# A graph network layer on one core: the normalise steps of the first stage in batches of eight blocks, the statistics further ahead, and x in twenty slots

## The chip, the cores and the metric

The kernel runs on 1 core of one Trainium2 chip. The metric is device time in microseconds (us) of one execution, lower is better.

## The reference, cut to what matters

`x` has 50,000 rows (nodes) of 128 features, and there are 12,500 edges (`src`, `dst`, sorted by `dst`), each with 3, 5 and 32 attributes. In the reference `rbf`, `pij` and `dij` are the edges' attributes, and each `_resmlp` is a two layer residual block of 128x128 matrices with its own weights.

```python
h = jnp.maximum(_layernorm(x, axis=-1), 0.0)
...
xx = _resmlp(h, ...[0])
xs, xp, xd = (_resmlp(h, ...[i])[idx_j] for i in (1, 2, 3))
s = xx + segment_sum(gs * xs, idx_i)
p = segment_sum(gp * xp[:, None, :], idx_i)
d = segment_sum(gd * xd[:, None, :], idx_i)
...
y = s + (pa * pb).sum(-2) + (da * db).sum(-2)
return x + _resmlp(y, ...[4])
```

The change lies in the first stage alone: `h`, the first MLP on every node, and the sorting of the edges.

## The kernel before, in words

The kernel has three stages that follow each other on every engine: `first_stage` (L265), `edge_phase` (L1014) and `final_stage` (L843).

**Work of the first stage.** The rows of x come in 98 blocks of 512 rows (`NB`, L93; `TB` = 4 rows in each of 128 partitions). For each block, x is loaded (`load_x`, L334, SP queue), VectorE takes the statistics of its four row groups (`stats`, L479, four `bn_stats`), a batch of blocks gets mean, 1/deviation and bias by 20 small VectorE instructions (`norm_step`, L488; LN_OPS = 20), and the rows are normalised and rectified: half by VectorE (`centre`, L537, and `rectify`, L548), half by ScalarE (`norm`, L699), except around the one-hots, where ScalarE does all four (`by_scalar`, L315). The block is stored as h (`store_h`, L350), TensorE transposes it (L780) and runs three layers (L795, L804, L811) with ScalarE's activations between (L723, L733, L739), and ScalarE copies the result out (L746) for `store` (L342).

**The sort.** Beside this the same engines sort the edges by source in two passes, first by the low digit, then by the high one. A pass starts with `digits` (L558) and 98 `onehots` (L587, VectorE), 49 in each of two steps; TensorE counts them (L755). Then 14 chunks of seven tiles follow, one every 2.5 steps: TensorE adds up running counts (L768), VectorE takes seven `picks` (L602, four in one step and three in the next) and one rank instruction (L619), and POOL scatters the rows to DRAM (L431), paced by TensorE's progress. Pass 0 has its one-hots at steps 0 and 1 and its chunks from step 4, pass 1 at steps 49 and 50 and from step 53 (`passes`, L271). Before pass 1, POOL reads the sorted edges back to SBUF in one DMA of 2 MB (L465), and `digits` of pass 1 waits for it (L565).

**What sets the order.** Every engine's program is written out by hand in steps k. On VectorE (L640 to L669) step k is: centre block k + 1; the statistics of the block or blocks of `stats_at(k)` (L299), with one norm step after each `bn_stats` from k = 7 on; rectify block k + 1, after the first block's statistics; the picks, then digits and one-hots, with norm steps between; and the norm steps left over. `stats_at(k)` is block k + 9 in the steady state. `norm_steps_at(k)` (L305) spreads the 20 steps of a batch of four blocks that begins at block b over k = b - 5 to b - 2, five a step. The centring of a block also waits for the transposition of the block four before it and for the store of that block's h (L543, L544).

x has 14 slots (`NX`, L96). Fourteen loads are issued at the start, the last six behind the loads of the edges (L380). Later, step k of SP stores h of block k, stores the result of block k - 4 and then loads block k + 12 (L407), whose slot was freed by block k - 2. So a block's x is asked for in SP's step k and its statistics stand in VectorE's step k + 3.

```python
            batches = [(0, 2), (2, 2)] + [(b, min(4, NB - b)) for b in range(4, NB, 4)]
...
                    if 0 <= k - 4 < NB:
                        store(k - 4)
                    if NX <= k + 12 < NB:
                        load_x(k + 12)
```

Of the kernel before, what the change touches and what calls it, by code (L numbers as in the profile page):

```python
# [76 lines left out]
def gnn_kernel(nc, x, src, dst, attr3, attr32, attr5, w_rs, w_rp, w_rd, w_pp, w_pd,  # L77
# [6 lines left out]
    P = 128  # L84
# [6 lines left out]
    TB = 4  # L91
    BLOCK = TB * P
    NB = -(-N // BLOCK)  # L93


    NX = 14  # L96
    CH = 7
    OH = 49
    T = -(-E // P)
# [25 lines left out]
    with ctx:  # L125
        def sb(name, shape, dt=fp32):
            return ctx.enter_context(nc.sbuf_tensor(name, shape, dt))
# [40 lines left out]

        xin = sb("xin", [P, NX, TB, F])
        yin = sb("yin", [P, 4, TB, F])  # L170
# [19 lines left out]
        def psb(name, shape, dt=fp32):  # L190
            return own.enter_context(nc.sbuf_tensor(name, shape, dt))
# [13 lines left out]
        upto = psb("upto", [P, LOW])  # L205
# [5 lines left out]
        earlier = psb("earlier", [P, CH, CH])  # L211
        corr = psb("corr", [P, T])
        warm = psb("warm", [P, 1])
        stat = psb("stat", [P, 16, TB, 6])
        lnt = psb("lnt", [P, 2, 6, 4 * TB])
        means = psb("means", [P, 2, 4 * TB])
        rnorm = psb("rnorm", [P, 2, 4 * TB])
        nbias = psb("nbias", [P, 2, 4 * TB])
        padrow = psb("padrow", [P, 3, W])

        groups = []
# [43 lines left out]
        def first_stage():  # L265
# [4 lines left out]
            BANK_A, BANK_COUNT, BANK_RUN, BANK_O = psum[3], psum[4], psum[5], psum[7]  # L270
            passes = (Pass(0, 0, 2, 4, 5, by_low), Pass(1, 49, 51, 53, 54, by_src))  # L271
            LN_OPS = 20
            batches = [(0, 2), (2, 2)] + [(b, min(4, NB - b)) for b in range(4, NB, 4)]

            x_in = [sem(f"n_x_in{i}") for i in range(NX)]
            stored = [sem(f"n_stored{i}") for i in range(4)]
# [22 lines left out]
            def stats_at(k):  # L299

                early = ((2, 3), (4, 5, 6, 7), (8, 9), (10, 11), (12, 13), (14,), (15,))
                blocks = early[k] if k < len(early) else (k + 9,)
                return [b for b in blocks if b < NB]

            def norm_steps_at(k):  # L305


                for B, (b, n) in enumerate(batches):
                    first, steps = ((0, 1), (0, 1), (1, 1), (3, 3))[B] if B < 4 else (b - 5, 4)
                    if B and first <= k < first + steps:  # L310
                        each = -(-LN_OPS // steps)
                        return [(B, i) for i in range(1, LN_OPS + 1) if (i - 1) // each == k - first]
                return []
# [19 lines left out]
            def sync(sp):  # L333
                def load_x(b):  # L334
                    s = b % NX
                    if b >= NX:
                        if by_vector(b - NX + 1):
                            sp.wait_ge(nrm_v, by_vector(b - NX + 1))
                        sp.wait_ge(nrm_a, b - NX + 1)
                    sp.dma_start(xin[:, s, :, :], xb_view(at(b), x)).then_inc(x_in[s], 16)  # L340

                def store(b):  # L342
                    s = b % 4
                    sp.wait_ge(row_done, b + 1)
                    if b == NB - 1:

                        sp.wait_ge(stored[(b - 1) % 4], 16 * ((b - 1) // 4 + 1))
                    sp.dma_start(xb_view(at(b), ysum), rowout[:, s, :, :]).then_inc(stored[s], 16)

                def store_h(b):  # L350
                    s = b % 4
                    sp.wait_ge(nrm_a, b + 1)
                    if by_scalar(b) < TB:
                        sp.wait_ge(nrm_v, by_vector(b + 1))
                    if b == NB - 1:

                        sp.wait_ge(h_stored[(b - 1) % 4], 16 * ((b - 1) // 4 + 1))
                    sp.dma_start(xb_view(at(b), htab), xn[:, s, :, :]).then_inc(h_stored[s], 16)

                load_x(0)  # L360
                load_x(1)
                sp.wait_ge(s_staged, 1)
                assert load_parts(src, st_src[:, :], sp, s_src, 1) == N_SRC
                sp.dma_start(w1_sb[:, m, :], w1[m, :, :]).then_inc(s_w, 16)
                with nc.allow_non_contiguous_dma(reason="biases to partitions"):
                    sp.dma_start(b1_sb[:, :], b1.rearrange("m k -> k m"), allow_slow_non_contiguous=True).then_inc(s_w, 16)
                    sp.dma_start(b2_sb[:, :], b2.rearrange("m k -> k m"), allow_slow_non_contiguous=True).then_inc(s_w, 16)
                load_x(2)
                load_x(3)
                sp.dma_start(w2_sb[:, m, :], w2[m, :, :]).then_inc(s_w, 16)  # L370
                sp.dma_start(wo_sb[:, m, :], wout[m, :, :]).then_inc(s_w, 16)
                for b in range(4, 8):
                    load_x(b)
                sp.wait_ge(s_staged, 2)
                n_rest = 0
                for dram, tile, per in ((dst, st_dst, 1), (attr3, st3, NP3), (attr5, st5, ND5), (attr32, st32, NRBF)):
                    flat = tile[:, :] if per == 1 else tile[:, :, :].rearrange("p t c -> p (t c)")
                    n_rest += load_parts(dram, flat, sp, s_edges, per)
                assert n_rest == N_REST
                for b in range(8, NX):  # L380
                    load_x(b)
                store_h(0)
                store_h(1)
                for k in range(2, NB + 4):
                    if k < NB:
                        store_h(k)
                    if k == 6:
                        sp.wait_ge(s_cst, 4)
                        sp.dma_start(w1_sb[:, m + 1:, :], w1[m + 1:, :, :].rearrange("m k n -> k m n")).then_inc(s_w2, 16)
                        sp.dma_start(w2_sb[:, m + 1:, :], w2[m + 1:, :, :].rearrange("m k n -> k m n")).then_inc(s_w2, 16)  # L390
                        sp.dma_start(wo_sb[:, m + 1:, :], wout[m + 1:, :, :].rearrange("m k n -> k m n")).then_inc(s_w2, 16)
                        sp.dma_start(wpp_sb[:, :], w_pp).then_inc(s_w2, 16)
                        sp.dma_start(wpd_sb[:, :], w_pd).then_inc(s_w2, 16)
                        for j in range(TB):
                            for n, w in enumerate((w_rp, w_rd, w_rs)):
                                sp.dma_start(wr_sb[j * Q:j * Q + NRBF, n, :], w).then_inc(s_w2, 16)
                    if k == 10:
                        for row, parts, each in groups:
                            sp.dma_start(by_src[row:row + parts * each, :].rearrange("(p t) w -> p t w", t=each),
                                         padrow[0:parts, 0:each, :]).then_inc(s_init, 16)  # L400
                        for lo in range(0, SPARE, TB):
                            n = min(TB, SPARE - lo)
                            sp.dma_start(ysum[N + lo * P:N + (lo + n) * P, :].rearrange("(t p) f -> p t f", p=P),
                                         zeros[:, 0:n * F].rearrange("p (t f) -> p t f", t=n)).then_inc(s_init, 16)
                    if 0 <= k - 4 < NB:
                        store(k - 4)
                    if NX <= k + 12 < NB:  # L407
                        load_x(k + 12)
                for s in s_scat:
                    sp.wait_ge(s, 2 * 16 * CHUNKS)  # L410
                sp.wait_ge(s_init, 16 * (-(-SPARE // TB) + len(groups)))
                with nc.allow_non_contiguous_dma(reason="one word of each row"):
                    for g in (0, 1):
                        load_group(sp, by_src, er, rb, nxt, g, g, TB, T, rows_in[g])
# [63 lines left out]
            def vector(dve):  # L478
                def stats(b, lo, hi):  # L479
                    s = b % NX  # L480
                    if lo == 0:
                        dve.wait_ge(x_in[s], 16 * (b // NX + 1))
                    for j in range(lo, hi):
                        last = nc.vector.bn_stats(stat[:, b % 16, j, :], xin[:, s, j, :])  # L484
                    if hi == TB:
                        last.then_inc(st_done, 1)

                def norm_step(B, i):  # L488


                    b, n = batches[B]
                    q, w, at0 = B % 2, n * TB, B * LN_OPS
                    st = stat[:, b % 16:b % 16 + n, :, :].rearrange("p b t c -> p (b t) c")
                    t = [lnt[:, q, i, 0:w] for i in range(6)]
                    mean, r, nb = means[:, q, 0:w], rnorm[:, q, 0:w], nbias[:, q, 0:w]
                    V_ = nc.vector
# [30 lines left out]
                    elif i == 19:  # L527
                        if B >= 2:
                            last = batches[B - 2][0] + batches[B - 2][1]
# [110 lines left out]
                for k in range(NB):  # L640
                    blocks, todo, pick = stats_at(k), norm_steps_at(k), picks_at(k)
# [1062 lines left out]
```

## Time and profile before

| what | value |
|---|---|
| median of 3 runs | 1262.18 us (1259.76 to 1266.66) |
| the profiled execution's own time | 1264.56 us |
| its span, first to last instruction | 1262.7 us |
| mean granted TensorE clock | 0.963 |
| VectorE busy in the span | 660.6 us (52%) |
| TensorE busy | 1135.0 us (90%) |
| first stage | from 0 to about 453 us of the span |

Busy shares are averages over three stages with different limits. A timeline row gives an instruction's start and duration, and in brackets the idle time of its engine before it and what ended that. The chain that ended last is followed back from the last instruction to what released each; "issue" in it is time without a cause that the profile shows. A wait for several semaphores is put down to the last of them by the profile, and the ends of matmuls are modelled.

### The profile page before, as it was taken

The numbers are of one execution on the slowest core, as the hardware profiler recorded it, in microseconds if no ns is written. First come the engines' busy times: TensorE is split into PE (matmuls) and PEld (weight loads), VectorE is DVE, ScalarE is ACT, GpSimd is POOL, SyncE is SP. The second block draws the span as 40 slices with busy tenths as digits, with TensorE's granted clock in tenths as the row PEclk, the third lists the DMA queues.
The fourth block names the chain that finished last, engine by engine and source line by source line (L and its number), as shares of the span: only waits on it lengthen the run. The fifth ranks groups of instructions, "written<-read, shape, count | busy, mean of one in ns | idle before, by whom it ended". The sixth has DMA issues, their size and how long they took to land.

```text
span 1262.7 us, 23295 instructions
## 1 busy us (share of the span) xinstructions
PE 1135.0 (90%) x6835; PEld 766.0 (61%) x6835; DVE 660.6 (52%) x2466; ACT 758.2 (60%) x1425; POOL 456.9 (36%) x423
## 2 busy tenths in 40 slices
PE   2778998797989856999999999999977999999998
PEld 1555665474656533666666666666744666666665
DVE  9866876695778303565556555655541222222222
ACT  2357878656877833555655565556524666666665
POOL 3055666015565531456555655565340000000000
PEclk9889999898999978999999999999988999999999
DMA  7166667735766430233333333333435888788876
GB/s 223 67 213 199 224 213 224 253 129 162 232 217 211 165 89 11 46 57 46 54 55 57 47 54 55 55 49 52 83 55 170 250 263 263 247 266 258 256 257 206
DMA packets 162765, 190.56 MB, mean 151 GB/s; under 512 B 57956, under 2 KB 82444, under 8 KB 162413
## 3 DMA queue, kind: packets, MB, share of 16 engines
q1 hardware_dynamic: 124636, 144.39, 38.4%
q0 software_dynamic: 23920, 19.29, 9.7%
q10 hardware_dynamic: 14112, 25.70, 5.3%
q8 instruction: 47, 0.77, 0.3%
q14 instruction: 50, 0.41, 0.1%
HBM read 93.01 MB, written 96.30 MB: 150 GB/s over the span
## 4 chain that ended last, share of the span: by engine, by line
PE 77%; DVE 11%; issue 7%; DMA 2%; ACT 1%; another core or an unknown queue 1%; SPq 0%; POOL 0%; ACTq 0%; POOLq 0%; DVEq 0%
PE bank L976 7%; PE quad L964 7%; PE bank L1489 5%; PE quad L968 5%; PE bank L1499 5%; PE bank L811 4%; PE quad L795 4%; PE bank L1563 4%; PE bank L1531 3%; DVE onehot L589 3%; PE bank L1564 3%; PE quad L804 3%; PE quad L956 3%; PE quad L780 2%; DVE stat L484 2%
## 5 line engine op out<-in xcount | busy, mean ns | idle before, releaser
L1164 POOL DMA_INDIRECT node_sums<-rowout,row_i x98 | 155.0, 1582 | 199.6 <-ACT rowout L1426 177.1
L900 DVE TENSOR_TENSOR rowout<-bank,xin 128x512 f32<-128x512 f32 x98 | 67.8, 692 | 242.0 <-PE bank L976 242.0
L811 PEld LDWEIGHTS bank<-wo_sb,s 128*128 128x128 f32 x784 | 102.8, 194 | 64.9 <-issue 64.9
L431 POOL DMA_INDIRECT edges_by_src<-pay,rank_i x98 | 96.2, 981 | 111.5 <-DVE rank_i L619 50.6
L431 POOL DMA_INDIRECT edges_by_low<-pay,rank_i x98 | 96.6, 986 | 99.3 <-DVE rank_i L619 42.2
L976 PEld LDWEIGHTS bank<-wo_sb,s 128*128 128x128 f32 x784 | 102.8, 191 | 47.8 <-issue 47.8
L1197 DVE SCALAR_TENSOR_TENSOR h<-bank,b_sb,hT 128x512 f32<-128x512 f32 (+1 forms) x75 | 55.5, 740 | 122.2 <-PE bank L1499 122.2
L484 DVE BATCH_NORM_STATS2 stat<-xin 128x6 f32<-128x128 f32 x392 | 105.4, 284 | 21.9 <-DMA xin<-in_x_dram 21.9
L811 PE MATMUL bank<-wo_sb,s 128*128 128x128 f32 x784 | 106.0, 279 | 11.0 <-issue 9.0
L72 POOL DMA_INDIRECT yin<-node_h,er x98 | 94.9, 968 | 53.8 <-issue 29.3
L709 ACT ACTIVATE xn<-xin,nbias,rnorm 128x128 f32<-128x128 f32 x210 | 101.8, 492 | 14.3 <-DVE nbias L535 14.3
L607 DVE SCALAR_TENSOR_TENSOR picked<-bank,onehot 128x256 bf16<-128x256 f32 x196 | 75.9, 418 | 62.8 <-issue 39.3
L795 PE MATMUL quad<-s,w_sb 128*128 128x512 f32 x196 | 105.6, 622 | 0.0
L976 PE MATMUL bank<-wo_sb,s 128*128 128x128 f32 x784 | 103.5, 275 | 0.9 <-DVE rowout L900 0.9
L964 PE MATMUL quad<-s,w_sb 128*128 128x512 f32 x196 | 101.4, 599 | 0.4 <-ACT s L919 0.4
L1373 ACT ACTIVATE s<-h 128x512 f32<-128x512 f32 (+1 forms) x75 | 46.6, 622 | 74.5 <-DVE h L1197 74.5
L1489 PE MATMUL bank<-s,w_sb 128*128 128x512 f32 (+1 forms) x150 | 79.9, 615 | 12.2 <-ACT s L1365 9.2
L1405 ACT COPY AB<-bank 128x512 f32<-128x512 f32 x98 | 58.1, 593 | 50.4 <-PE bank L1564 50.2
L780 PE MATMUL quad<-ident,xn 128*128 128x128 f32 x296 | 47.8, 286 | 40.8 <-issue 21.7
L746 ACT COPY rowout<-bank 128x512 f32<-128x512 f32 x98 | 57.5, 587 | 43.6 <-remote 27.8
L919 ACT ACTIVATE s<-quad,b_sb 128x512 f32<-128x512 f32 x98 | 67.3, 687 | 26.3 <-PE quad L964 26.2
L733 ACT ACTIVATE s<-quad,b_sb 128x512 f32<-128x512 f32 x98 | 67.2, 686 | 22.6 <-PE quad L795 14.4
(193 smaller groups left out, 2376.1 us busy)
## 6 DMA issues: line engine op xcount, KB each, us to landing
xin<-in_x_dram SPq DMA_DIRECT2D x196, 256.0 KB, 3.9
node_h<-xn SPq DMA_DIRECT2D x98, 256.0 KB
node_sums<-rowout SPq DMA_DIRECT2D x98, 256.0 KB
yin<-node_sums SPq DMA_DIRECT2D x98, 256.0 KB, 4.0
out_dram<-rowout ACTq DMA_DIRECT2D x98, 256.0 KB, 3.8
border_sums_by_tile<-border_sums SPq DMA_DIRECT2D x24, 256.0 KB, 2.1
pay<-edges_by_low POOLq DMA_DIRECT2D x1, 2058.0 KB, 10.7
edges_by_low<-pay,rank_i POOLq DMA_INDIRECT x98
```

The source lines that it names most:

```text
L72: pool.indirect_dma_start(out=xg[:, s, j, :], out_offset=None, in_=x, in_offset=bass.IndirectOffsetOnAxis(ap=er[:, s, j, 1:2].bitcast(mybi ...
L431: nc.gpsimd.indirect_dma_start(out=ps.dram, out_offset=bass.IndirectOffsetOnAxis(ap=rank_i[:, t:t + 1], axis=0), in_=pay[:, t, :], in_offs ...
L484: last = nc.vector.bn_stats(stat[:, b % 16, j, :], xin[:, s, j, :])
L607: nc.vector.scalar_tensor_tensor(out=picked[:, j, :], in0=BANK_RUN[:, 0:LOW], scalar=1.0, in1=onehot[:, t, :], op0=ALU.mult, op1=ALU.mult, ...
L709: ins = nc.scalar.activation(xn[:, b % 4, j, :], xin[:, s, j, :], ACT.Relu, bias=nbias[:, q, i:i + 1], scale=rnorm[:, q, i:i + 1])
L780: last = nc.tensor.matmul(BANK_X[k % 4][:, j * P:(j + 1) * P], xn[:, k % 4, j, :], ident[:, :], start=j == 0, stop=False, is_transpose=Tru ...
L795: nc.tensor.matmul(BANK_A[:, :], w1_sb[:, m, :], s1[:, (k - 1) % 3, :], start=True, stop=True).then_inc(a_done, 1)
L811: last = nc.tensor.matmul(BANK_O[:, j * P:(j + 1) * P], s3[:, (k - 3) % 3, j * P:(j + 1) * P], wo_sb[:, m, :], start=True, stop=True)
L964: nc.tensor.matmul(BANK_A[:, :], w1_sb[:, m, :], s1[:, s, :], start=True, stop=True).then_inc(a_done, 1)
L976: last = nc.tensor.matmul(BANK_O[:, j * P:(j + 1) * P], s3[:, s, j * P:(j + 1) * P], wo_sb[:, m, :], start=True, stop=True)
L1164: nc.gpsimd.indirect_dma_start(out=ysum, out_offset=bass.IndirectOffsetOnAxis(ap=row_i[:, t % 2, j:j + 1], axis=0), in_=urow[:, t % 2, j, ...
L1489: nc.tensor.matmul(BANK_A[:, 0:e], w1_sb[:, MLP[m], :], s1[:, k % 2, 0:e], start=True, stop=True).then_inc(a_done, 1)
```

## The change

There are four edits, all in `first_stage`.

```diff
-    NX = 14
+    NX = 20
...
-        stat = psb("stat", [P, 16, TB, 6])
-        lnt = psb("lnt", [P, 2, 6, 4 * TB])
+        stat = psb("stat", [P, 32, TB, 6])
+        lnt = psb("lnt", [P, 2, 6, 8 * TB])
...
-            batches = [(0, 2), (2, 2)] + [(b, min(4, NB - b)) for b in range(4, NB, 4)]
+            LARGE = 32
+            batches = [(0, 2), (2, 2)] + [(b, 4) for b in range(4, LARGE, 4)] + [(b, min(8, NB - b)) for b in range(LARGE, NB, 8)]
...
-                blocks = early[k] if k < len(early) else (k + 9,)
+                upto = [k + 9 + min(max(k - 7, 0) // 2, 5) for k in (k - 1, k)]
+                blocks = early[k] if k < len(early) else range(upto[0] + 1, upto[1] + 1)
...
-                    first, steps = ((0, 1), (0, 1), (1, 1), (3, 3))[B] if B < 4 else (b - 5, 4)
+                    first, steps = ((0, 1), (0, 1), (1, 1), (3, 3))[B] if B < 4 else (b - 5, 4) if b <= LARGE else (b - 6, 5)
...
-                    if NX <= k + 12 < NB:
-                        load_x(k + 12)
+                    if NX <= k + NX - 2 < NB:
+                        load_x(k + NX - 2)
```

`means`, `rnorm` and `nbias` grow like `lnt`, and the other places where `stat` is indexed take `% 32`. What the edits do:

- Batches hold eight blocks from block 32 on. Their 20 norm steps stand in VectorE's steps k = b - 6 to b - 2, four a step, and the three steps after that have none. Each works on 32 elements per partition and no longer on 16.
- The statistics run ahead by 14 blocks in place of 9. The lead grows by one block in each of the steps 9, 11, 13, 15 and 17, which take the statistics of two blocks. In return the last five steps that had statistics have none.
- x has 20 slots. Twenty loads are issued at the start, and SP's step k loads block k + 18. A block's x is asked for four steps ahead of its statistics.

The first place is VectorE ahead of the second pass's one-hots: the end of step 48 and step 49. `digit_i` is the first instruction of `digits`. Before:

```order
L484 BN_STATS stat<-xin 128x6
L522 TENSOR_TENSOR lnt<-lnt 128x16
L484 BN_STATS stat<-xin 128x6
L524 TENSOR_TENSOR lnt<-lnt 128x16
L484 BN_STATS stat<-xin 128x6
L526 SCALAR_TENSOR_TENSOR lnt<-lnt 128x16
L484 BN_STATS stat<-xin 128x6
L522 TENSOR_TENSOR lnt<-lnt 128x16
L566 CAST digit_i<-pay 128x98
L568 TENSOR_SCALAR digit_i<-digit_i 128x98
L571 CAST digit_f<-digit_i 128x98
L589 TENSOR_SCALAR onehot<-digits_h,digit_f 128x256 x2
```

Now (two lines more stand above, so line numbers are higher by 2):

```order
L547 TENSOR_TENSOR xn<-xin,means 128x256
L486 BN_STATS stat<-xin 128x6 x4
L556 SCALAR_TENSOR_TENSOR xn<-xn,rnorm 128x256
L547 TENSOR_TENSOR xn<-xin,means 128x256
L486 BN_STATS stat<-xin 128x6 x4
L556 SCALAR_TENSOR_TENSOR xn<-xn,rnorm 128x256
L486 BN_STATS stat<-xin 128x6 x4
L568 CAST digit_i<-pay 128x98
L570 TENSOR_SCALAR digit_i<-digit_i 128x98
L573 CAST digit_f<-digit_i 128x98
L591 TENSOR_SCALAR onehot<-digits_h,digit_f 128x256 x49
```

The steps `lnt<-lnt` between the statistics are gone in steps 47, 48 and 49 and between the one-hots of step 49; step 50 has the first four of the batch at block 56.

The second place is SP's queue at the start: the last load of the edges, the x loads behind it and the first stores of h. Before:

```order
L239 DMA st<-in_edge_attr_dram 15x3136
L239 DMA st<-in_edge_attr_dram 1x1728
L340 DMA xin<-in_x_dram 128x512 x6
L358 DMA node_h<-xn 128x512 x3
L340 DMA xin<-in_x_dram 128x512
L358 DMA node_h<-xn 128x512
```

Now:

```order
L239 DMA st<-in_edge_attr_dram 15x3136
L239 DMA st<-in_edge_attr_dram 1x1728
L342 DMA xin<-in_x_dram 128x512 x12
L360 DMA node_h<-xn 128x512 x3
L342 DMA xin<-in_x_dram 128x512
L360 DMA node_h<-xn 128x512
```

Six more loads of x stand ahead of the first store of h, and each later load is for a block that is six further on.

## Rows read from the trace of the kernel before

**Rows 1.** The page: busy time by engine, and the chain that ended last
```profile
PE 1135.0 (90%) x6835; PEld 766.0 (61%) x6835; DVE 660.6 (52%) x2466; ACT 758.2 (60%) x1425; POOL 456.9 (36%) x423
...
PE 77%; DVE 11%; issue 7%; DMA 2%; ACT 1%; another core or an unknown queue 1%; SPq 0%; POOL 0%; ACTq 0%; POOLq 0%; DVEq 0%
```

**Rows 2.** Timeline of TensorE after the first stage: start, duration, what, [idle before]
```profile
464.91 1.08 PE L1468 MATMUL quad<-ident,yin 128*128 128x128 f32 x4 [12.19 <-DMA yin<-node_h,er]
```

**Rows 3.** Stretches: length, busy PE, PEld, DVE, ACT, POOL, clock, DMA share, GB/s
```profile
225.00:250.00 25.00, 16.00 (x84) 10.57 (x83) 15.26 (x85) 17.60 (x37) 0.59 (x1) 0.87 0.76 275
...
350.00:375.00 25.00, 21.43 (x118) 14.38 (x117) 17.55 (x103) 18.41 (x38) 15.21 (x16) 1.00 0.65 210
```

**Rows 4.** Timeline of VectorE, 225 to 250 us
```profile
225.97 0.42 DVE L545 TENSOR_TENSOR xn<-xin,means 128x256 f32<-128x256 f32 x1
...
227.34 0.29 DVE L484 BATCH_NORM_STATS2 stat<-xin 128x6 f32<-128x128 f32 x1 [0.95 <-DMA xin<-in_x_dram]
...
237.62 0.29 DVE L484 BATCH_NORM_STATS2 stat<-xin 128x6 f32<-128x128 f32 x1 [8.69 <-DMA xin<-in_x_dram]
...
238.74 0.24 DVE L566 CAST digit_i<-pay 128x98 int32<-128x98 f32 x1
...
239.52 0.48 DVE L589 TENSOR_SCALAR onehot<-digits_h,digit_f 128x256 bf16<-128x256 bf16 x2
```

**Rows 5.** Timeline of the SP queue, same stretch
```profile
224.68 0.40 SPq L340 DMA_DIRECT2D xin<-in_x_dram  x1
...
227.72 0.69 SPq L340 DMA_DIRECT2D xin<-in_x_dram  x1
```

**Rows 6.** The reload of the sorted edges: POOL's timeline, and issue to landing
```profile
225.90 0.59 POOL L465 DMA_DIRECT2D pay<-edges_by_low  x1 [2.40 <-DMA edges_by_low<-pay,rank_i]
...
pay<-edges_by_low POOLq DMA_DIRECT2D x1, 2058.0 KB, 10.7
```

**Rows 7.** Timeline of TensorE around the one-hots of step 49
```profile
239.14 0.66 PE L780 MATMUL quad<-ident,xn 128*128 128x128 f32 x4 [0.31 <-ACT xn L709]
...
239.63 1.02 PE L795 MATMUL quad<-s,w_sb 128*128 128x512 f32 x2
...
249.35 1.04 PE L755 MATMUL bank<-onehot,ident_h 128*128 128x256 bf16 x4 [8.69 <-DVE onehot L589]
```

**Rows 8.** The chain that ended last, 223 to 300 us: start, duration, what
```profile
250.88 9.22 DVE onehot L589 x47
...
260.15 5.52 PE bank L755 x49
```

**Rows 9.** Timeline of VectorE: statistics alone, with a step between, and two picks
```profile
52.17 0.86 DVE L484 BATCH_NORM_STATS2 stat<-xin 128x6 f32<-128x128 f32 x4
...
92.65 0.42 DVE L607 SCALAR_TENSOR_TENSOR picked<-bank,onehot 128x256 bf16<-128x256 f32 x1 [0.99 <-PE bank L768]
...
114.35 0.42 DVE L607 SCALAR_TENSOR_TENSOR picked<-bank,onehot 128x256 bf16<-128x256 f32 x1 [1.18 <-issue]
...
154.65 0.29 DVE L484 BATCH_NORM_STATS2 stat<-xin 128x6 f32<-128x128 f32 x1
...
154.94 0.28 DVE L484 BATCH_NORM_STATS2 stat<-xin 128x6 f32<-128x128 f32 x1
```

**Rows 10.** The stretch 12 to 16 us, columns as in Rows 3
```profile
12.00:16.00 4.00, 1.09 (x4) 0.71 (x4) 3.93 (x24) 2.73 (x7) 0.00 (x0) 1.00 1.04 291
```

**Rows 11.** Timeline of VectorE in the first one-hot stage
```profile
14.31 0.47 DVE L589 TENSOR_SCALAR onehot<-digits_h,digit_f 128x256 bf16<-128x256 bf16 x2
...
23.29 5.36 DVE L589 TENSOR_SCALAR onehot<-digits_h,digit_f 128x256 bf16<-128x256 bf16 x9
```

**Rows 12.** Timeline of ScalarE in the second pass: a late copy
```profile
333.27 0.59 ACT L746 COPY rowout<-bank 128x512 f32<-128x512 f32 x1 [1.93 <-remote]
```

**Rows 13.** Timeline of TensorE in the second pass, after an idle stretch
```profile
311.24 0.63 PE L780 MATMUL quad<-ident,xn 128*128 128x128 f32 x4 [2.13 <-issue]
...
311.71 1.84 PE L795 MATMUL quad<-s,w_sb 128*128 128x512 f32 x2
```

More of the change, by code:

```diff
@@ L213, in gnn_kernel @@
         warm = psb("warm", [P, 1])
-        stat = psb("stat", [P, 16, TB, 6])
-        lnt = psb("lnt", [P, 2, 6, 4 * TB])
-        means = psb("means", [P, 2, 4 * TB])
-        rnorm = psb("rnorm", [P, 2, 4 * TB])
-        nbias = psb("nbias", [P, 2, 4 * TB])
+        stat = psb("stat", [P, 32, TB, 6])
+        lnt = psb("lnt", [P, 2, 6, 8 * TB])
+        means = psb("means", [P, 2, 8 * TB])
+        rnorm = psb("rnorm", [P, 2, 8 * TB])
+        nbias = psb("nbias", [P, 2, 8 * TB])
         padrow = psb("padrow", [P, 3, W])
@@ L483, in stats @@
                     for j in range(lo, hi):
-                        last = nc.vector.bn_stats(stat[:, b % 16, j, :], xin[:, s, j, :])
+                        last = nc.vector.bn_stats(stat[:, b % 32, j, :], xin[:, s, j, :])
                     if hi == TB:
@@ L492, in norm_step @@
                     q, w, at0 = B % 2, n * TB, B * LN_OPS
-                    st = stat[:, b % 16:b % 16 + n, :, :].rearrange("p b t c -> p (b t) c")
+                    st = stat[:, b % 32:b % 32 + n, :, :].rearrange("p b t c -> p (b t) c")
                     t = [lnt[:, q, i, 0:w] for i in range(6)]
```

## The prediction

> **What bounds the kernel now.** I read the page first. TensorE is busy 90% of the span and 77% of the chain that ended last; VectorE is busy 52% and has 11% of that chain [rows 1]. The change adds and removes nothing on TensorE, so what it can move is TensorE's idle time in the first stage. The handover at the stage's end keeps nothing back: the next stage's first transposition comes 12.19 us after TensorE's last work, behind stores, loads of edge rows and a gather that all follow the last block [rows 2]. Time won in the first stage is time won in all.
>
> Next I read stretches of the first stage. In one from the second pass VectorE is busy 17.55 us of 25 and TensorE 21.43. In 225 to 250 us TensorE has its worst stretch of the sorting time, 16.00 of 25, at a mean granted clock of 0.87, with DMA at 0.76 [rows 3].
>
> The timelines say why. VectorE centres block 49 at 225.97 and does the statistics of step 48 at 227.34. Then it waits 8.69 us, to 237.62, for the x of block 58. Then come four statistics with four norm steps between, `digits` at 238.74 and the first one-hot at 239.52 [rows 4]. That x was asked for at 227.72 [rows 5], so it took 9.9 us; the median over the kernel is 3.9 (the page's DMA issues). Two us earlier, at 225.90, POOL had asked for the 2 MB of sorted edges, which took 10.7 us [rows 6]. TensorE transposes block 50 at 239.14, does a little more and then waits 8.69 us for the one-hots of step 49, to 249.35 [rows 7]. The chain runs through both sets of one-hots and the second set's counts [rows 8]. So the one-hots' start at 239.52 sets the rest of the stage, and each us off it is a us won.
>
> **The change, part by part.**
>
> *The x of step 49 comes earlier.* The statistics of step 49 are now those of block 63, whose load stands in SP's step 45. That is the load at 224.68, where block 57 stood before, and not the one at 227.72 [rows 5]. Block 57's data let VectorE go on at 227.34, so it landed in 2.7 us [rows 4, 5], issued 1.2 us ahead of the reload [rows 6]. VectorE then has nothing to wait for until `digits`, which waits for the reload: 225.90 + 10.7 = 236.6 [rows 6]. Four statistics without steps take 0.86 us [rows 9], so even with centring and rectifying before them they end near 229. `digits` moves from 238.74 to 236.6: 2.1 us. That is far less than the 8.69 us of the wait, because the reload is late next, 1.0 us ahead of where the x had been. The 1.1 us of statistics and steps that stood behind the wait now lie under the reload's.
>
> *The norm steps.* From block 32 on there were 17 batches and are now 9, so 8 x 20 = 160 instructions go. One step between two statistics stretches their distance from 0.86 / 4 = 0.21 us to 154.94 - 154.65 = 0.29 us [rows 9], so it costs 0.08 us, and 160 come to 12.8 us. The steps that stay from there on, 9 x 20, are longer, since they work on 32 elements and not on 16: 16 more are at most 16/256 of a centring of 256 elements, 0.42 us [rows 4], so 0.03 us each and some 5 us in all, an estimate. So VectorE loses some 8 us of work. What of it is on the path? One step among the first set of one-hots is: 0.1 us. The others lie where VectorE waits for TensorE: it waits for running counts ahead of nearly every chunk, for instance 0.99 and 1.18 us [rows 9], and most other such waits in the second pass are longer. I take 0.1 us. The bounds are 0 and, if all of the second pass were on VectorE's path, 4 us: steps 53 to 86 had 34 x 5 = 170 norm steps and now have 88; 82 x 0.08 = 6.6, less 88 x 0.03 = 2.6.
>
> *The statistics further ahead.* Five steps of the first pass take four more statistics each, 0.86 us [rows 9], 4.3 us together. In the steps 9, 11, 13, 15 and 17 they stand in front of a wait for TensorE: of the five waits the two shortest are 0.99 us (step 11) and 1.18 us (step 16, behind step 15) [rows 9], both longer than 0.86. I take 0; the upper end is 4.3. The last five steps without statistics give nothing back, since VectorE has time there.
>
> *Six more loads at the start.* They add 6 x 256 KB to a queue that moves 291 GB/s [rows 10], so 5.3 us of transfers, and six issues ahead of the first store of h. The edges' loads stand ahead of them and are not delayed. h is needed by nobody before block 4. Does a busy DMA slow VectorE? At a DMA share of 1.04 [rows 10] two one-hots take 0.47 us [rows 11], which is their time at 239.52 as well, 0.48 [rows 4]. But nine of them at 23.29 took 5.36 us [rows 11], where 9 x 0.2 = 1.8 was due. The DMA was busy then too, and POOL was copying the edges. I take 0, by the row with the same DMA share and no POOL work. If it was the DMA, 5.3 us more at a third of the pace cost 3.5 us; that is the upper end.
>
> *More slots in the steady state.* The loads per step are the same three transfers, so shares don't change; an earlier x only matters where VectorE waits for it, which outside the stretch above happens off the path.
>
> **The sum.** -2.1 (x under the reload) - 0.1 (a step) = -2.2 us. Against the profiled execution's own time, 1264.56, that is 1262.4 (span 1260.5). That execution was 2.4 us above the median of the three runs, 1262.18; against the median it is 1260.0.
>
> **A rule against the trace.** VectorE's idle time in the second pass [rows 3] and its waits ahead of the picks [rows 9] say that fewer small steps there are worth nothing. The Trainium skill (Perfetto Trace Analysis, section "Optimizing Scalar/DVE Operations") says that each VectorE instruction on SBUF has some 60 ns of fixed overhead and that grouping into larger operations improves throughput if the engine is saturated. By that figure, as an estimate, the 160 instructions carry 9.6 us; the trace's 0.08 us per step is of the same size. By the rule the gain would come in time only if VectorE were saturated, which is the first rival.
>
> **The rivals.**
>
> *Faster: VectorE was on the path in the second pass.* The chain gives it 11% [rows 1], and several of its pieces are picks and statistics of the second pass. Against it: TensorE's idle stretches there begin mostly with a late copy on ScalarE, as 1.93 us at 333.27, whose release the profile puts down to none of VectorE's work [rows 12]. If the 4 us above all counted: 1262.2 - 2.2 - 4 = 1256.0; with a clock dip of TensorE that no longer comes (1.6 us, below) 1254.4. I put the case at 1255.
>
> *Slower: the double statistics delay TensorE in the first pass.* The place is steps 9 to 17. It decides once 0.86 us no longer fit into VectorE's wait, and in two of the five cases there is only 0.13 and 0.3 us to spare [rows 9]. The price is 4.3 us, and each idle stretch that it makes can cost clock: after 2.1 us of idle time the next matmuls of L795 took 1.84 us [rows 13] where 1.02 is their time at the higher clock [rows 7]. L804 behind them is the same work, so such a dip costs some 1.6 us. With three dips: 4.3 + 4.8 - 2.2 = +6.9, so 1269.1.
>
> *No change: the reload is the clock of step 49 in full.* Its landing time of 10.7 us comes from one transfer [rows 6], and x loads and stores share its engines. If they reach it otherwise in the new order and it lands near 238.7, nothing of the 2.1 us is left: 1262.
>
> **How the numbers follow.** The forecast has 0.60, VectorE on the path 0.20, no change 0.12, slower 0.08. A measurement of this kernel can tell about 0.5%, 6.3 us, from no change, so faster means under 1255.9 and slower over 1268.5. The forecast and no change lie within it. Of the faster rival's 0.20 three quarters, 0.15, lie below 1255.9, since the case sits just under it, and the forecast's lower edge adds 0.05: 0.20. Slower has 0.08, the rest is 0.72. The range: down to 1253.5, which takes in the faster rival and the scatter of runs (2.4 us below and 4.5 above the median before), and up to 1265.5, which takes in no change, the same scatter and the six loads' upper end against the gain.
>
> **What would show it.** Right: VectorE's wait for x near 228 us is gone, a wait for the reload stands in front of `digits`, `digits` starts about 2 us earlier against the reload's issue, TensorE's wait for the one-hots shrinks from 8.69 to some 6.6 us, and VectorE's busy time falls by more than 8 us while the steps between L780's transpositions in the second pass stay at their length. Wrong: a shorter second pass (from the one-hots to the end) by over 3 us would be the faster rival; waits of TensorE on VectorE around steps 10 to 19 the slower one; a stall of VectorE in the first one-hots until the x loads have landed would make the six loads the cost.

## The result, and the profile after

The changed kernel takes 1258.96 us (median of 22 runs, 1255.45 to 1262.05), the kernel before 1261.93 us on the same chip (22 runs, 1258.41 to 1266.66). The ratio is 0.9974, with a 95% interval of 0.9964 to 0.9983: 3.3 us less, between 2.1 and 4.5 (the medians are 3.0 apart). The forecast was 2.2 us less.

| | before | after |
|---|---|---|
| profiled span | 1262.7 us | 1256.3 us |
| VectorE busy, instructions | 660.6 us, 2466 | 647.9 us, 2306 |
| TensorE busy | 1135.0 us | 1131.0 us |
| chain: TensorE, VectorE | 77%, 11% | 77%, 10% |
| VectorE's waits for x | 21.9 us | 1.3 us |
| reload, issue to landing | 10.7 us | 9.3 us |
| first conversion of `digits`, from the reload's issue | 12.84 us | 9.28 us |
| the same, from the reload's landing | 2.2 us | 0.0 us |
| TensorE's wait for the one-hots of step 49 | 8.69 us | 4.69 us |

All line numbers of the change are two higher than those of before from the norm steps on. VectorE's timeline of the changed kernel around step 49, the answer to [rows 4] (start us, us, engine, line, operation, idle time ahead and what ended it):

```profile
221.72 0.86 DVE L486 BATCH_NORM_STATS2 stat<-xin 128x6 f32<-128x128 f32 x4
222.50 0.41 DVE L556 SCALAR_TENSOR_TENSOR xn<-xn,rnorm 128x256 f32<-128x256 f32 x1
224.21 0.87 DVE L486 BATCH_NORM_STATS2 stat<-xin 128x6 f32<-128x128 f32 x4 [1.31 <-DMA xin<-in_x_dram]
231.32 0.25 DVE L568 CAST digit_i<-pay 128x98 int32<-128x98 f32 x1 [6.24 <-DMA pay<-edges_by_low]
```

The last wait for x ahead of `digits` is 1.31 us where it was 8.69, and the reload now stands ahead of `digits`. POOL's timeline has its issue, and the page's DMA issues its landing, 9.3 us (last column):

```profile
222.04 0.58 POOL L467 DMA_DIRECT2D pay<-edges_by_low  x1 [2.00 <-DMA edges_by_low<-pay,rank_i]
```

```profile
pay<-edges_by_low POOLq DMA_DIRECT2D x1, 2058.0 KB, 9.3
```

TensorE's timeline there, beside [rows 7]:

```profile
235.64 0.65 PE L782 MATMUL quad<-ident,xn 128*128 128x128 f32 x4 [0.23 <-ACT xn L711]
236.13 1.02 PE L797 MATMUL quad<-s,w_sb 128*128 128x512 f32 x2
241.85 8.09 PE L757 MATMUL bank<-onehot,ident_h 128*128 128x256 bf16 x49 [4.69 <-DVE onehot L591]
...
251.53 0.60 PE L782 MATMUL bank<-ident,xn 128*128 128x128 f32 x4
...
260.14 0.60 PE L782 MATMUL quad<-ident,xn 128*128 128x128 f32 x4
```

**Where the time went between the two profiles.** Follow the start of TensorE's transposition of a block in both. Block 3: 52.37 before, 50.72 after. Block 50: 239.14 and 235.64, 3.5 us apart. Block 51: 258.59 and 251.53, 7.1 us apart. Block 97: 443.11 and 437.99, 5.1 us apart. So the pair gained 3.6 us at the one-hots of step 49, as much again ahead of it, and gave 2 us back in the second pass, where TensorE stood still 5.67 and 4.13 us ahead of two transpositions (at 283.62 and 306.91) and before 5.01 and 2.13. Two single profiles differ by 6.4 us here and the medians by 3; what of each piece is the change's had to be found by experiment. Of the 3.6 us, 2.2 are that `digits` no longer stands behind the reload's landing, and 1.4 that this one reload took 9.3 us and not 10.7.

### The profile page after: what moved, and what is told of

It reads as the page before. It is cut to its first block, busy times and chain, and to the rows that moved or that the text cites. A ratio compares the mean times of both kernels' runs of the same rounds, so it can differ in the third digit from the quotient of the medians.

```text
span 1256.3 us, 23121 instructions
## 1 busy us (share of the span) xinstructions
PE 1131.0 (90%) x6835; PEld 764.7 (61%) x6835; DVE 647.9 (52%) x2306; ACT 757.4 (60%) x1425; POOL 459.3 (37%) x423
## 4 chain that ended last, share of the span: by engine, by line
PE 77%; DVE 10%; issue 8%; DMA 2%; another core or an unknown queue 1%; ACT 1%; POOL 0%; SPq 0%; DVEq 0%; POOLq 0%; ACTq 0%
PE bank L978 7%; PE quad L966 7%; PE bank L1491 5%; PE quad L970 5%; PE bank L1501 5%; PE bank L813 4%; PE bank L1565 4%; PE quad L797 4%; PE bank L1533 3%; PE bank L1566 3%; PE quad L806 3%; PE quad L958 3%; DVE onehot L591 3%; PE quad L782 2%; PE quad L1575 2%
## 5 line engine op out<-in xcount | busy, mean ns | idle before, releaser
L486 DVE BATCH_NORM_STATS2 stat<-xin 128x6 f32<-128x128 f32 x392 | 99.6, 282 | 1.3 <-DMA xin<-in_x_dram 1.3
L748 ACT COPY rowout<-bank 128x512 f32<-128x512 f32 x98 | 57.4, 586 | 42.6 <-remote 25.7
```

Of the source, the lines that this page charges most:

```text
L486: last = nc.vector.bn_stats(stat[:, b % 32, j, :], xin[:, s, j, :])
```

## The experiments

Theory A is the prediction's: x asked for earlier takes the x's wait out of step 49, and the reload is late next. Theory B puts the gain down to the norm steps, Theory C a part to the six early loads. Each kernel was measured beside the kernel before on its own chip.

**E1: before, with one slot more.** `load_x` four steps ahead of the statistics instead of three:

```diff
-    NX = 14
+    NX = 15
-                    if NX <= k + 12 < NB:
-                        load_x(k + 12)
+                    if NX <= k + NX - 2 < NB:
+                        load_x(k + NX - 2)
```

> The kernel before with one slot more for x (15), so that x is asked for four steps ahead of its statistics and not three; batches of four and statistics nine ahead stay. Theory A (the gain is the x of step 49, which no longer waits behind the reload): the 8.69 us wait for x near 228 us is gone or under 2 us, a wait for the reload stands ahead of digits, TensorE's wait for the one-hots falls to 4.5 to 7 us, and the time is 2 to 4 us under the kernel before, as the full change. Theory B (the gain comes from the norm steps of the larger batches): within 1 us of the kernel before. Theory C (part of it, 1.65 us by block 3, comes from the six early loads): here block 3's transposition stays within 0.5 us of where it was in the kernel before, at 52.4, since there is only one load more.

**E2: the same with `NX = 20`.**

> The kernel before with 20 slots for x, and so six more loads at the start and x asked for nine steps ahead of its statistics; batches of four and statistics nine ahead stay. Theory A: as the full change, 3 us under the kernel before, and no x wait near 228 us; the reload then decides. Theory B (norm steps): within 1 us of before. Theory C (the early loads themselves move the first one-hots): the transposition of block 3 comes at about 50.7 us, 1.65 us earlier than in the kernel before, as in the full change; if that was chance it stands anywhere between 50.5 and 52.5.

**E3: the changed kernel with `NX = 19`,** so that the lead is three steps again.

> The changed kernel with 19 slots for x: x is asked for three steps ahead of its statistics, as in the kernel before; all else of the change stays. Theory A: the x of step 49 is again the load issued after the reload; VectorE waits 6 to 9 us for it near 228 us, TensorE's wait for the one-hots is back at 7 to 9 us, and the time is 2 to 3.5 us over the changed kernel, about that of the kernel before. Theory B: within 1 us of the changed kernel.

**E4: the changed kernel with batches of four throughout:**

```diff
-            batches = [(0, 2), (2, 2)] + [(b, 4) for b in range(4, LARGE, 4)] + [(b, min(8, NB - b)) for b in range(LARGE, NB, 8)]
+            batches = [(0, 2), (2, 2)] + [(b, min(4, NB - b)) for b in range(4, NB, 4)]
```

> The changed kernel with batches of four blocks throughout (160 norm steps more, each some 0.03 us shorter); statistics fourteen ahead and 20 slots stay. Theory A, with norm steps hidden as predicted: VectorE's busy time rises by about 12 us and the kernel's time by 0 to 0.5 us. Theory B: VectorE's steps are on the path and the time goes back to that of the kernel before, 3 us more.

All four ran on one chip, against 34 runs of the kernel before (1194.43 us; this chip is 5% quicker, of which below). The ratios: E1 0.9973 (0.9960 to 0.9986), E2 0.9981 (0.9970 to 0.9992), E3 0.9997 (0.9987 to 1.0008), E4 0.9982 (0.9971 to 0.9994). One slot in the kernel before gives as much as the full change gave on its chip. Theory B falls as the only cause: E4 has the 160 norm steps back (VectorE busy 658.4 us, 2466 instructions) and keeps 2.2 us. Theory C falls too: block 3's transposition came at 52.09 in E1, 51.78 in E2, 52.25 in E3, which has five early loads, and 50.63 in E4. It takes values from 50.6 to 52.4 whatever the number of loads (50.78 in the kernel before itself, in E5's profile below), so the 1.65 us between the two first profiles need no cause.

Two expectations failed in what the profiles show. In E1 the reload does stand ahead of `digits`, but it took 11.7 us, and TensorE's wait for the one-hots is 8.95 us, where 4.5 to 7 were expected:

```profile
207.35 0.25 DVE L566 CAST digit_i<-pay 128x98 int32<-128x98 f32 x1 [9.76 <-DMA pay<-edges_by_low]
```

```profile
217.96 7.79 PE L755 MATMUL bank<-onehot,ident_h 128*128 128x256 bf16 x49 [8.95 <-DVE onehot L589]
```

And E3 had no x wait of 6 to 9 us, but 1.76 us ahead of the last statistics before `digits`, and then the reload. SP's queue and POOL's timeline say why: the x was asked for 1.7 us ahead of the reload and landed in 2.8 us, so E3 didn't bring back the wait that it was made for.

```profile
199.56 0.87 DVE L486 BATCH_NORM_STATS2 stat<-xin 128x6 f32<-128x128 f32 x4 [1.76 <-DMA xin<-in_x_dram]
...
208.12 0.26 DVE L568 CAST digit_i<-pay 128x98 int32<-128x98 f32 x1 [7.69 <-DMA pay<-edges_by_low]
```

```profile
196.76 0.41 SPq L342 DMA_DIRECT2D xin<-in_x_dram  x1
```

```profile
198.47 0.59 POOL L467 DMA_DIRECT2D pay<-edges_by_low  x1 [2.77 <-DMA edges_by_low<-pay,rank_i]
```

**E5: the kernel before, and E6: the change, both unedited, for their profiles on this chip.**

> The kernel before, unchanged, on this chip, for its profile: the experiments ran on a chip where the blocks of the first stage follow each other faster (3.05 us and not 3.8 at places). Both theories expect the time of the kernel before. What it should show: whether VectorE's x wait of step 49 (8.69 us in the first profile) is there too, and how long TensorE waits for the one-hots: Theory A wants 8 us or more here, and 9 to 12 if the reload lands as late as in the kernel with 15 slots (11.7 us).

> The full change, unchanged, on this chip. Theory A: as the kernel before with 20 slots and the changed kernel with batches of four, 2 to 3 us under the kernel before (ratio 0.9975 to 0.9985), with the reload's wait ahead of digits. If norm steps counted as well (Theory B as a part), under those two by another 1 us or more.

E5 took 1.0006 of the kernel before (0.9991 to 1.0021), as it must. E6 took 0.9998 (0.9982 to 1.0015): here the full change gained nothing that can be seen, against 0.9974 on the first chip and 0.9975 to 0.9985 expected. Two lines of VectorE's timeline in the kernel before (E5), then one of POOL's and one of VectorE's in the change (E6):

```profile
204.90 0.29 DVE L484 BATCH_NORM_STATS2 stat<-xin 128x6 f32<-128x128 f32 x1 [7.98 <-DMA xin<-in_x_dram]
...
206.02 0.25 DVE L566 CAST digit_i<-pay 128x98 int32<-128x98 f32 x1
```

```profile
196.15 0.58 POOL L467 DMA_DIRECT2D pay<-edges_by_low  x1 [3.06 <-DMA edges_by_low<-pay,rank_i]
```

```profile
206.70 0.25 DVE L568 CAST digit_i<-pay 128x98 int32<-128x98 f32 x1 [10.46 <-DMA pay<-edges_by_low]
```

In E5 the reload was issued at 194.77 and landed 9.9 us later, at 204.6; x landed 0.3 us behind it, where the first chip had 1.0 us between the two. So `digits` stood 1.4 us behind the landing in E5 and 0.0 us in E6: the change takes away 1.4 us here and not 2.2. And in E6 the reload was issued 1.3 us later, 20.15 us after block 40's transposition against 18.84. That is so for every kernel with statistics fourteen ahead on this chip (E3 21.23, E4 20.19, E6 20.15, E7 20.18), and for none with nine (E1 18.93, E2 18.76, E5 18.84, E8 19.26). On the slower chips there is no such split (21.68 in the kernel before and 21.22 in E12; 20.58 in the change, 21.25 in E9, 22.13 in E10, 21.42 in E11). In E6 POOL's last scatter ahead of the reload ends later than in E5 and lands later behind that (POOL waits 3.06 us for it and not 2.67); by what way the statistics do that wasn't tried and stays open.

The six profiles of this chip that have the reload in one piece:

| | lead of x (steps), statistics | ratio | reload took | `digits` behind its landing | TensorE's wait |
|---|---|---|---|---|---|
| E5 | 3, nine ahead | 1.0006 | 9.9 us | 1.4 us | 8.34 us |
| E1 | 4, nine | 0.9973 | 11.7 | 0.0 | 8.95 |
| E2 | 9, nine | 0.9981 | 8.9 | 0.0 | 5.97 |
| E3 | 3, fourteen | 0.9997 | 9.6 | 0.0 | 9.04 |
| E4 | 4, fourteen | 0.9982 | 11.0 | 0.0 | 9.49 |
| E6 | 4, fourteen | 0.9998 | 10.5 | 0.0 | 8.85 |

1.4 us off by the earlier x and 1.3 us on by the later reload would explain E6 and E3, which are alike in time (1193.73 and 1194.28 us) though x is asked for four steps ahead in one and three in the other. So E3 doesn't show that taking the lead away takes the gain away. But E4 has the later reload too and is at 0.9982, and E1 gained more than 1.4 us. A single profile can't settle it: the reload's own time differs by 2.8 us between them, and E5's was its fastest run, 4.4 us below its median. What is shown on this chip is that the earlier x alone (E1, E2) makes the kernel faster; that it does so by this wait isn't shown here, and why E6 gained nothing stays open. The intervals of E4 and E6 overlap, so these runs don't show that large batches cost anything.

**E7: the change with the reload in two halves side by side; E8: the same in the kernel before.** `digits` is made for tiles 0 to 48 ahead of step 49's one-hots and for 49 to 97 ahead of step 50's:

```diff
-                nc.gpsimd.dma_start(pay[:, :, :], by_low.rearrange("(p t) w -> p t w", t=T)).then_inc(s_back, 16)
+                nc.gpsimd.dma_start(pay[:, 0:OH, :], by_low.rearrange("(p t) w -> p t w", t=T)[:, 0:OH, :]).then_inc(s_back, 16)
+                nc.gpsimd.dma_start(pay[:, OH:T, :], by_low.rearrange("(p t) w -> p t w", t=T)[:, OH:T, :]).then_inc(s_back2, 16)
...
+                        lo, hi = (OH, T) if late else (0, OH)
+                        dve.wait_ge(s_back2 if late else s_back, 16)
```

> The changed kernel with the reload as two transfers, tiles 0 to 48 and 49 to 97, and digits of each half made before its own set of one-hots. Theory A (the reload decides once x is early): the first half lands 4 to 6 us after the issue and not 9 to 12, TensorE's wait for the first one-hots falls to 0 to 3 us, and the time is 3 to 5 us under the changed kernel. Rival (the two transfers share the engines evenly and land together, or something else bounds the one-hots, such as the step's own place behind the row of blocks): within 1 us of the changed kernel.

> The kernel before with the same split reload; x is still asked for three steps ahead. Theory A: the x of step 49 now decides alone, asked for behind the reload; it lands no sooner by much, so the gain over the kernel before is 0 to 2 us, less than half of what the split gives on the changed kernel. Rival (x was never the cause, only the reload): the same 3 to 5 us as on the changed kernel.

E7 took 0.9964 (0.9949 to 0.9978), 2.95 us under E6's median; E8 0.9988 (0.9973 to 1.0003). In E7 the first half landed 7.3 us after its issue, where 4 to 6 were expected, and TensorE's wait is 5.55 us and not 0 to 3. In E8 VectorE went on waiting for x, 5.12 us, and `digits` followed that x at 204.77, with its half of the reload there for 1.3 us. The split took 0.34% off the change (E6 to E7) and 0.12% off the kernel before, as Theory A has it: the two late transfers hide each other, and cutting one pays in full only once the other is early. The intervals overlap, though, and TensorE's wait in E8's profile is no longer than in E7's, 5.36 us, so these two runs suggest it and don't show it.

**E9: E7 with the halves in turn,** the second issued when the first has landed:

```diff
                 pool.wait_ge(s_back, 16)
+                nc.gpsimd.dma_start(pay[:, OH:T, :], by_low.rearrange("(p t) w -> p t w", t=T)[:, OH:T, :]).then_inc(s_back2, 16)
```

> The changed kernel with the split reload, and the second half issued only when the first has landed (in the side-by-side split the first half took 7.3 us). Theory A: alone on its queue the first half lands 4.5 to 6 us after its issue, TensorE's wait for the first one-hots falls by another 2 us against the side-by-side split (5.55 us to 3 to 4), the second half lands in time for the second set, and the time is 4 to 6 us under the kernel before. Rival (the reload is held up by the loads and stores of x, h and the rows, so that half of it takes no less when the other half is away): the first half takes 7 us again and the time is that of the side-by-side split, 3.8 us under before.

**E10: E9, and the one-hots reported and counted seven at a time, in both passes:**

```diff
+                        if n % CH == CH - 1:
+                            last.then_inc(s_oh, 1)
-                    last.then_inc(s_oh, 1)
...
-                    pe.wait_ge(s_oh, ps.n * (T // OH) + g + 1)
                     for t in ps.made(ps.onehots + g):
+                        if t % CH == 0:
+                            pe.wait_ge(s_oh, ps.n * CHUNKS + t // CH + 1)
```

> The one before with a finer signal: VectorE reports its one-hots seven at a time and TensorE counts them seven at a time, and not 49. If the way from the reload through the one-hots to their counts is what sets step 49 (Theory A), the 5.5 us of counts now lie beside the making of the one-hots, but for the last seven: 4 to 5 us less in the second sorting pass for the first set, as much again in the first pass if its one-hots bound TensorE there too, so 8 to 15 us under the kernel before. Rival (TensorE idles then for another reason, such as its own clock after small pieces of work, or VectorE's wait for the counts): less than 2 us under the split reload alone.

**E11: the full change a third time.**

> The full change once more. Its first measurement was 0.9974 of the kernel before, where blocks came at a slower pace, and the second 0.9998 on the chip of the experiments, where x and the reload landed 0.2 us apart before the change. Theory A, with the gain being the distance from the reload's landing to the x's: 0.998 to 1.000 where the pace is the fast one (0 to 2 us), 0.996 to 0.998 where it is the slow one. If the second measurement was chance: 0.9975 here too.

These three ran on a chip of the slower pace (the kernel before: 1266.40 us, 17 runs). E9 took 0.9945 (0.9928 to 0.9963), E10 0.9890 (0.9874 to 0.9906), E11 0.9979 (0.9960 to 0.9997). Against the kernel before that is 7.7, 13.4 and 3.0 us by the medians, for E9 more than the 4 to 6 expected and for E10 within the 8 to 15. E10, at 1253.03 us, has the lowest ratio of the study. POOL's timeline in E11, VectorE's and TensorE's below it:

```profile
224.72 0.58 POOL L467 DMA_DIRECT2D pay<-edges_by_low  x1 [2.57 <-DMA edges_by_low<-pay,rank_i]
```

```profile
226.39 0.87 DVE L486 BATCH_NORM_STATS2 stat<-xin 128x6 f32<-128x128 f32 x4 [0.22 <-DMA xin<-in_x_dram]
235.58 0.25 DVE L568 CAST digit_i<-pay 128x98 int32<-128x98 f32 x1 [8.31 <-DMA pay<-edges_by_low]
```

```profile
246.11 7.98 PE L757 MATMUL bank<-onehot,ident_h 128*128 128x256 bf16 x49 [6.89 <-DVE onehot L591]
...
255.68 0.60 PE L782 MATMUL bank<-ident,xn 128*128 128x128 f32 x4
256.11 1.02 PE L797 MATMUL quad<-s,w_sb 128*128 128x512 f32 x2
256.97 5.51 PE L757 MATMUL bank<-onehot,ident_h 128*128 128x256 bf16 x49
```

Here the reload took 10.8 us, as in the kernel before (10.7), and this is nearly the forecast's case: `digits` 10.86 us after the issue against 12.84 (2.0 us won, 2.1 forecast), TensorE's wait 6.89 us (6.6 forecast). But 0.9979 doesn't tell the two readings apart that E11 was run for: it lies in the 0.996 to 0.998 expected of a chip of this pace, and its interval also holds the 0.9975 expected if E6 was chance. E9 cut the wait to 2.56. Its first half landed 6.6 us after the issue, so half the bytes take more than half the time of the 10.8. E8's first half took 6.6 us too, with the second beside it, so that the halves in turn are quicker than side by side isn't shown; the intervals of E7 and E9, from two chips, overlap. In E10 TensorE has no wait for the first set at all:

```profile
234.96 1.02 PE L806 MATMUL quad<-s,w_sb 128*128 128x512 f32 x2
235.82 5.51 PE L766 MATMUL bank<-onehot,ident_h 128*128 128x256 bf16 x49
241.17 1.02 PE L815 MATMUL quad<-s,w_sb 128*128 128x512 f32 x2
```

From block 50's transposition to block 52's it took 20.7 us (234.47 to 255.20), E11 26.6, E9 22.9. That is 2.2 us of the 5.7 that E10 gained over E9. The larger part lies in the first pass, whose one-hots are reported by sevens too: block 3's transposition comes at 47.41 us in E10 and 51.57 in E9, outside the 50.6 to 52.4 of all profiles without this edit, and at 47.68 in E12.

**E12: the kernel before with E10's two edits and nothing of the change.**

> The kernel before with both edits of the fastest kernel so far (split reload with its halves in turn, one-hots reported by sevens), and nothing of the change: fourteen slots, batches of four, statistics nine ahead. On the changed kernel the two edits gave 0.989 of the kernel before. Theory A: with the reload's first half early, the x of step 49, asked for behind it, is what VectorE waits for (5 to 8 us), the one-hots start 2 to 4 us later against the reload's issue than in the kernel with all three, and the ratio to before is 0.991 to 0.993: the change is worth 3 to 5 us here. Rival (the change is worth nothing where the pace is the fast one, or the x no longer waits once the reload is halved): within 0.1% of the kernel with all three on the same kind of chip, no x wait over 2 us near step 49.

It took 0.9927 (0.9913 to 0.9941), 1252.10 us, on another chip of the slower pace (the kernel before there: 1261.59 us). VectorE's timeline:

```profile
226.86 0.30 DVE L487 BATCH_NORM_STATS2 stat<-xin 128x6 f32<-128x128 f32 x1 [4.66 <-DMA xin<-in_x_dram]
...
227.98 0.20 DVE L573 CAST digit_i<-pay 128x49 int32<-128x49 f32 x1
```

The reload was issued at 219.04, so `digits` came 8.94 us after it, where E10 has 6.73 (222.20 to 228.93): 2.2 us of the 4.7 us between 0.9927 and 0.9890. The first half took 6.5 us here and 6.7 in E10, so the difference is the x and not the reload: `digits` stands 2.4 us behind the landing in E12 and 0.0 in E10. The rest of the 4.7 us lies outside this place and wasn't followed. The ratio is as Theory A had it. The two ratios come from two chips, each against its own baseline, and their intervals don't meet; but E12's own median is 0.9 us below E10's, so the worth of the change here rests on the two baselines, which are 4.8 us apart.

## Why the prediction was right, point by point

- **The x of step 49 under the reload, -2.1 us.** Right in place, order and size on the slower chips: the wait for x went, the reload stood next, and `digits` moved from 2.2 us behind the reload's landing to 0.0 (first pair and E11; with the reload halved, 2.4 in E12 and 0.0 in E10). E1 shows by time that an earlier x alone makes the kernel faster, though on the quick chip, where its profile doesn't show TensorE's wait shrinking. That `digits` moved by 3.6 us against the reload's issue in the first pair, and TensorE's wait to 4.69 us where 6.6 were forecast, is in part luck: that reload landed in 9.3 us. The prediction took 10.7 us from one transfer and said so; over nine profiles with the reload in one piece it took 8.9 to 11.7 us, with no order by kernel. The sum of 2.2 us lies near the lower end of the measured 2.1 to 4.5; whatever is above it wasn't traced to a place.
- **A step among the one-hots, and the norm steps, -0.1 us.** Not contradicted; no run takes the norm steps off alone. VectorE's busy time fell by 12.7 us, more than the 8 forecast, since the 5 us for the longer steps were an upper bound. E4 puts those steps back and is no slower than E6, so they lie beside TensorE's work. The Trainium skill's rule on grouping small VectorE operations (Perfetto Trace Analysis, section "Optimizing Scalar/DVE Operations") holds on its own condition: VectorE is at 52%, not saturated.
- **Double statistics in steps 9 to 17, 0.** TensorE's waits show nothing of them on the first chip: ahead of the picks VectorE still waits 6.04, 2.75 and 0.82 us (at 82.83, 103.27 and 111.34; before 7.69, 5.21 and 1.18). On the quick chip the reload is issued about 1.3 us or more later in all kernels that have them, which the prediction did not foresee; by what way is open.
- **Six early loads, 0.** Right: E2 (six) gives no more and no less than E1 (one), within their intervals.
- **The rivals.** *VectorE on the path*: the second pass was no shorter, 186.5 us from block 51's transposition to block 97's against 184.5 before, and E4 speaks against it. *Slower by double statistics*: not seen. *No change, the reload being the clock in full*: E6 looks like it, in time and in its profile, where the reload is issued later and lands 0.7 us after `digits` began in E5. But E1, E2 and E4 gained on the same chip, so the chip alone doesn't decide it.
- **What it left out.** A long idle stretch of TensorE has a second price: the 49 counts behind it took 7.65 us before, 8.09 after, 7.98 in E11 (6.8 to 8.1 in the twelve profiles that have the wait), and 5.51 where TensorE had been busy. The length of the wait hardly matters: behind E9's 2.56 us they took 7.19, behind E6's 8.85 us 6.82. That price was not in the sum and did not need to be, since the wait only shrank. It belongs in the sum where a wait disappears, as in E10.

## What to carry to other kernels

When a wait ends on a late transfer, look for the next late one and the distance between them: that distance, not the wait, is the most that can be won there. Here it was 2.2 us of an 8.69 us wait, and 1.4 us in the profile from the quick chip. Try the smallest edit alone: one slot more in the kernel before gave 0.9973, and twenty slots, fourteen blocks of lead and larger batches together 0.9974 and 0.9979 at the slower pace and 0.9998 on the chip where the single slot was tried. And when one engine makes many small things that another consumes, try the signal's grain: seven at a time instead of 49 took another 0.55% off, where the halved reload ahead of it had taken 0.34%.

## What the runs showed of the hardware

- **Chips differ by 5% on this kernel, and not by the clock alone.** The kernel before took 1261.93, 1266.40 and 1261.59 us in three sets of runs and 1194.43 and 1194.59 us in two sets on the chip of E1 to E8. The mean granted clock was 0.967 in E11's profile and 0.978 in E6's. The same 50 us of the first stage, windows of the change on a slower chip (E11) and the quick one (E6):

```profile
130.00:180.00 50.00, 45.19 (x243) 30.33 (x243) 37.00 (x203) 38.48 (x78) 29.61 (x30) 1.00 0.69 218
```

```profile
130.00:180.00 50.00, 50.00 (x279) 35.04 (x277) 42.06 (x220) 46.00 (x92) 38.71 (x38) 1.00 0.81 253
```

  The columns are window, length, busy us of TensorE, its weight loads, VectorE, ScalarE and POOL, then granted clock, DMA share and GB/s. The clock is 1.00 in both, but on the slower chip TensorE is idle a tenth of this stretch. ScalarE's copies of the rows (L748) stand behind idle time of 6.9 us in this stretch there, 5.4 of it with a release that the trace doesn't name, and of 1.1 us on the quick chip, while one copy takes the same 587 and 585 ns. What that release is stays open.
- **Idle time and the granted clock.** In E11 the granted clock from 246 to 254 us, right behind TensorE's 6.89 us of idle time, is 0.68 as a mean over the stretch, so part of it was at the lower level of 1.2 GHz; in E10, where the wait is gone, it is 1.00 from 234 to 260 us:

```profile
246.00:254.00 8.00, 7.89 (x50) 6.14 (x51) 8.00 (x44) 0.00 (x0) 0.00 (x0) 0.68 0.00 1
```

```profile
234.00:260.00 26.00, 22.98 (x160) 16.89 (x159) 25.76 (x123) 13.20 (x28) 0.00 (x0) 1.00 0.42 157
```

- **A 2 MB reload beside x, h and row traffic** takes 8.9 to 11.7 us, and its first half 6.5 to 6.7 us alone on its queue (E9, E10, E12) and 6.6 and 7.3 us beside the other half (E8, E7).
